# Unread products after each exposed recurrence step, with the last projection spread over four steps

## The reference, cut to what matters

```python
def step(carry, xs):
    h, c = carry
    xi_t, xf_t, xg_t, xo_t = xs
    i_t = jax.nn.sigmoid(xi_t + h @ V_i)
    g_t = jnp.tanh(xg_t + h @ V_c)
    o_t = jax.nn.sigmoid(xo_t + h @ V_o)
    c_new = h * c + i_t * g_t
    h_new = o_t * jnp.tanh(c_new)
    return ((h_new, c_new), h_new)
```

## Time and profile before

| | us |
|---|---|
| median of 3 runs (lowest, highest) | 839.23 (838.78, 840.98) |
| the profiled execution, its own time | 840.06 |
| its span, first to last instruction | 838.3 |
| PE busy, PEld busy | 688.0, 408.7 |
| DVE busy, ACT busy, POOL busy | 519.1, 372.2, 229.7 |
| chain that ended last | PE 57%, DVE 25%, ACT 8%, issue 5% |
| mean granted clock of TensorE | 0.851 |

### The profile page before, as it was taken

The page is one execution under the profiler, slowest core; times in us unless marked ns, Lnnn a source line. Parts: engine busy times, 40 slices in busy tenths (PEclk is TensorE's granted clock), DMA queues, the critical chain, the costliest instruction groups (busy, mean ns, idle before and its releaser), DMA issues.

```text
span 838.3 us, 16451 instructions
## 1 busy us (share of the span) xinstructions
PE 688.0 (82%) x6414; PEld 408.7 (49%) x6414; DVE 519.1 (62%) x1098; ACT 372.2 (44%) x693; POOL 229.7 (27%) x203
## 2 busy tenths in 40 slices
PE   3677778854579999988897899979899998787775
PEld 3674545633442222245233344246667775565553
DVE  3865775568956555366457666548776773465543
ACT  2232444431415456645444555545565654333332
POOL 4156754574600032111024110304332332000000
PEclk9989689866559999999999999988999998555555
DMA  9840000000025333200232132200000000000000
GB/s 184 144 80 10 1 1 1 2 0 1 0 99 173 103 128 124 72 2 7 79 106 67 61 98 81 60 1 2 2 2 2 2 2 1 11 10 9 11 10 12
DMA packets 42402, 36.85 MB, mean 44 GB/s; under 512 B 20888, under 2 KB 29848, under 8 KB 42328
## 3 DMA queue, kind: packets, MB, share of 16 engines
q1 hardware_dynamic: 41242, 35.57, 16.1%
q10 hardware_dynamic: 1088, 0.26, 0.2%
HBM read 33.85 MB, written 1.97 MB: 43 GB/s over the span
## 4 chain that ended last, share of the span: by engine, by line
PE 57%; DVE 25%; ACT 8%; issue 5%; POOL 2%; DMA 2%; ACTq 0%; DVEq 0%; SPq 0%; POOLq 0%
PE PS L1644 10%; PE PS L1631 10%; PE PS L1607 6%; PE PS L1679 3%; PE PS L1746 3%; PE PS L1735 3%; PE PS L1658 3%; DVE XC L980 3%; PE PS L1593 2%; PE PS L1700 2%; DVE st L962 2%; PE PS L1714 2%; ACT Y L696 2%; DVE st L978 2%; ACT LS L855 2%
## 5 line engine op out<-in xcount | busy, mean ns | idle before, releaser
L1644 PE MATMUL PS<-Y,W1f 64*128 64x512 f32 x384 | 111.5, 660 | 4.9 <-DVE Y L1121 2.8
L1631 PE MATMUL PS<-XC,w2s 128*64 128x512 f32 x384 | 105.8, 631 | 1.2 <-ACT BIG L732 1.2
L1607 PE MATMUL PS<-LS,V 64*64 64x32 f32 x1140 | 70.8, 270 | 36.1 <-DVE LS L1263 36.1
L1607 PEld LDWEIGHTS PS<-LS,V 64*64 64x64 f32 x1140 | 58.7, 188 | 70.6 <-DVE LS L1263 62.4
L741 ACT ACTIVATE XC<-PS 128x1024 f32<-128x1024 f32 x68 | 69.3, 1022 | 51.2 <-PE PS L1631 41.7
L600 POOL TENSOR_TENSOR st<-st,mhalf 128x8 f32<-128x8 f32 x12 | 21.6, 1796 | 194.1 <-DVE st L1108 194.1
L1121 DVE TENSOR_TENSOR Y<-XD,UF 128x512 f32<-128x512 f32 x96 | 65.3, 692 | 14.5 <-DMA UF<-gd 9.0
L1631 PEld LDWEIGHTS PS<-XC,w2s 128*64 128x64 f32 x384 | 19.6, 138 | 76.3 <-issue 66.6
L1250 DVE SCALAR_TENSOR_TENSOR LS<-LS 128x32 f32<-128x32 f32 x96 | 19.8, 206 | 57.5 <-ACT LS L849 39.7
L1644 PEld LDWEIGHTS PS<-Y,W1f 64*128 64x128 f32 x384 | 30.6, 190 | 50.1 <-issue 31.7
L178 POOL TENSOR_TENSOR st<-st,mhalf 128x8 f32<-128x8 f32 x24 | 39.3, 1639 | 36.6 <-DVE st L965 36.6
(11 more groups left out here) (236 smaller groups left out, 1437.5 us busy)
## 6 DMA issues: line engine op xcount, KB each, us to landing
UF<-gd SPq DMA_DIRECT2D x192, 128.0 KB, 2.9
BIG<-in_x SPq DMA_DIRECT2D x8, 512.0 KB, 12.7
out<-X SPq DMA_DIRECT2D x48, 32.0 KB, 2.0
W1f<-in_L_ffn_w SPq DMA_DIRECT2D x2, 512.0 KB, 6.3
EX<-in_L_ffn_w SPq DMA_DIRECT2D x1, 1024.0 KB, 15.1
H<-in_txt SPq DMA_DIRECT2D x2, 256.0 KB, 12.4
w2s<-in_L_ffn_w SPq DMA_DIRECT2D x1, 512.0 KB, 9.3
gd<-EX SPq DMA_DIRECT2D x6, 64.0 KB, 1.7
```

What stands on the lines that cost most here:

```text
L1607: mm = pe.matmul(PS[r, b, o:o + HN], V3[r, g, :], HB[r, (t - 1) % 4, :], start=False, stop=True, skip_group_check=True)
L1631: mm = pe.matmul(PS[64 * h:64 * h + 64, 6, :], w2s[:, 2 * p + h, :], Hb[:, n % 2 * 2 + h, :], start=(p == 0), stop=(p == E // 2 - 1))
L1644: mm = pe.matmul(PS[:, n % 2 * 2 + h, :], W1f[r, 2 * p + h, :], Rb[r, n % 4, :], start=True, stop=True)
```

## The change

It does these things:

- **Unread products.** At the end of PE's slot, for steps 32 to 94, one more fp32 product of 128 x 128 weights (`W1f`) with 256, 480, 176 or 272 columns (by t % 4), written to PSUM bank 0 or 1 and read by nobody. In the six steps in which PE also transposes a part of chunk 4 or 5, it is 288 columns shorter.
- **The last projection.** `project` in step 32 is replaced by one of its four products in each of steps 33, 37, 41 and 45 (`last_project`, bank 1), and `o_out` in step 32 by two halves in steps 46 and 47 (`last_out`).
- **Parts of chunks.** Chunks 4 and 5 begin at slots 114 and 130 (steps 49 and 65) in place of 108 and 124, with their parts spread further; chunk 3's last parts, the turn and the two copies, go from unit 26 to unit 24 of the attention. The parts of the last experts' chunk are spread otherwise over the first units.
- **Hidden steps.** They begin one slot later. On DVE `weigh` now comes between `cell` and `hidden`.
- **A wait.** In slot 50 PE's wait for the first attention's end comes behind `up`.

```diff
-        TAIL_DVE = {0: (2, 3, 4, 5), 1: (6, 7), 2: (8, 9), 3: (10,), 4: (11, 12), 5: (13, 14)}
-        TAIL_POOL = {1: ("pw0", "mu0", "ga"), 4: ("pw1", "mu1")}
-        TAIL_ACT = {1: 0, 4: 1}
+        TAIL_DVE = {0: (2, 3), 1: (4, 5), 2: (6, 7), 3: (8, 9, 10), 4: (11, 12), 5: (13, 14)}
+        TAIL_POOL = {2: ("pw0", "mu0", "ga"), 4: ("pw1", "mu1")}
+        TAIL_ACT = {2: 0, 4: 1}
...
-        LS0 = 3 * E + 10
+        LS0 = 3 * E + 11
...
-            if j == 1 and p in ("out", "t0", "t1", "k13", "k14"):
+            if j in (1, 4) and p in ("out", "t0", "t1", "k13", "k14"):
...
-        XB = (3 * E + 2, 3 * E + 13, None, None, NPR + 12, NPR + 28)
-        XALONE = dict(ao0=0, r0=0, q0=1, ao1=2, r1=2, q1=3, n0=4, n1=5, sq=6, n2=7, n3=7, pw=7, ones=8, mu=9, turn=10, c0=10, c1=11)
-        XLATER = dict(ao0=0, ao1=1, r0=0, q0=0, r1=1, q1=1, n0=1, n1=1, ones=2, sq=2, n2=3, n3=3, pw=3, mu=4, turn=5, c0=5, c1=5)
+        XB = (3 * E + 2, 3 * E + 13, None, None, NPR + 18, NPR + 34)
+        XALONE = dict(ao0=0, r0=0, q0=1, ao1=4, r1=4, q1=5, n0=6, n1=7, sq=8, n2=9, n3=9, pw=9, ones=10, mu=11, turn=12, c0=12, c1=12)
+        XLATER = dict(ao0=0, ao1=1, r0=0, q0=0, r1=1, q1=1, n0=2, n1=2, ones=3, sq=3, n2=4, n3=4, pw=4, mu=5, turn=7, c0=7, c1=7)
...
-              3: dict(ao0=16, r0=16, q0=16, ao1=20, r1=20, q1=20, n0=21, n1=22, sq=22, n2=23, n3=23, pw=23, mu=23, ones=24, turn=26, c0=26, c1=26)}
+              3: dict(ao0=16, r0=16, q0=16, ao1=20, r1=20, q1=20, n0=20, n1=21, sq=21, n2=22, n3=22, pw=22, mu=22, ones=23, turn=24, c0=24, c1=24)}
...
+        LAST_O = [XS + 1 + 4 * c for c in range(NP)]
+        LAST_C = [LAST_O[-1] + 1, LAST_O[-1] + 2]
...
+            def last_out(h):
+                R, G, b0 = UNITS[-1][0:3]
+                b0 = b0 // GA * GA + h * (GA // 2)
+                act.wait_ge(S("a_o"), G + 1)
+                act.activation(AO[:, :].rearrange("p (t b) -> p b t", b=NB)[:, b0:b0 + GA // 2, RB * R:RB * R + RB],
+                               PS[:, 1, 256 * h:256 * h + 256].rearrange("p (b i) -> p b i", i=RB), ACT.Identity, bias=bus[:, 0:1]).then_inc(S("o_ev"), 1)
...
-                if g == LS1:
-                    o_out(len(UNITS) - 1)
+                if t in LAST_C:
+                    last_out(LAST_C.index(t))
...
                 if t is not None:
                     cell(t)
+                if ahead <= g + 2 < NPR and not (g in AT or g + 1 in AT):
+                    weigh(g + 2)
+                if t is not None:
                     hidden(t)
                     if t % 4 == 1 and t > 4 and not begins(g - 1):
                         output(t // 4 - 1)
-                if ahead <= g + 2 < NPR and not (g in AT or g + 1 in AT):
-                    weigh(g + 2)
...
-                pe.wait_ge(S("o_ev"), 4 * (c // 2) + 4)
+                pe.wait_ge(S("o_ev"), 4 * (c // 2) + 4 + (c // 2 == NR - 1))
...
+            def last_project(c):
+
+                u, G = len(UNITS) - 1, NG - 1
+                mm = pe.matmul(PS[64 * (c % 2):64 * (c % 2) + 64, 1, :], NPt[:, c, :], Zs[G % 2][:, :, RB * c:RB * c + RB],
+                               start=(c < 2), stop=(c >= 2))
+                if c == NP - 1:
+                    mm.then_inc(S("a_o"), 1)
...
-                    if t == XS:
-                        project(NG - 1, len(UNITS) - 1, 2 * NG)
+                    if t in LAST_O:
+                        last_project(LAST_O.index(t))
...
+                if g >= LS1 and t < T - 1:
+
+                    n = (256, 480, 176, 272)[t % 4] - (288 if residual(g, "ao0", "ao1", "turn") else 0)
+                    b = 0 if t <= LAST_C[-1] + 1 else 1
+                    pe.matmul(PS[:, b, 0:n], W1f[:, 0, :], w2s[:, 0:8, :].rearrange("p e d -> p (e d)")[:, 0:n], start=True, stop=True)
```

More of the change, by code:

```diff
@@ L1576, in gates_x @@
                     if 4 * k == XS + 4:
-                        pe.wait_ge(S("o_ev"), NG)
+                        pe.wait_ge(S("o_ev"), NG - 1)
                     if k >= 2:
@@ L1841, in _ @@
                     pe.wait_ge(S("u_ev0"), 2 * G)
[L1842 to L1846, removed]
                 if t:
@@ L1853, in _ @@
                         out_tp(t // 4 - 1)
-                    if t == XS:
-                        project(NG - 1, len(UNITS) - 1, 2 * NG)
+                    if t in LAST_O:
+                        last_project(LAST_O.index(t))
                 if g < NPR and g not in (AT[0] + 1, AT[0] + 2):
                     up(g)
+                if g == AT[0] + 3:
+                    pe.wait_ge(S("z_ev0"), (JOBS[units_of(0)[-1] + 1] + 1) // 2)
+                    pe.wait_ge(S("z_ev1"), JOBS[units_of(0)[-1] + 1] // 2)
+                    pe.wait_ge(S("o_ev"), NB // GA)
                 if 2 <= g < NPR and not begins(g) and not begins(g - 1):
```

## The result

The changed kernel takes 845.22 us, median of 20 runs (838.68 to 850.29). The kernel before, beside it on the same chip, takes 839.39 us (835.49 to 846.10, 20 runs). The ratio is 1.0063, interval 1.0042 to 1.0084: slower by 0.6%. The ratios are of fast runs: those of the experiments leave out the profiled run and any that is more than 1.5% above the kernel's fastest. The profiled execution took 845.52 us, its span is 843.8 us.

What follows compares the result with a forecast made beforehand. The exposed steps were taken as bound by the chain, with PE's narrow products slowed at 1.2 GHz. The terms summed to +28.3, or 868.4 us; -6.6 for ten faster steps gave 862 us, range 821 to 870.

Steps and rivals of the forecast that it cites:

- rival B: Exposed steps: the clock alternates, half of the steps at each level, 846 us (835 to 855); chance 0.15.
- I expect the exposed part to start low, as it does now: Start of the exposed steps: the clock is at 1.2 GHz there, because the attention ends in a sparse stretch.
- I give them ten of the steps: Exposed steps: ten find the clock raised and cost about 1.71 us instead of 2.37, so -6.6 us.
- part 1: Chunk 3's turn and copies two units earlier: PE's wait at the start of the exposed part goes, -2.0 us.
- Part 3: Unread products at 1.2 GHz: they stand in front of the next gates, +28.4 us over 63 steps.
- Part 2: Projection out of step 32: the 5.21 us to the next h become an ordinary step, -3.3 us.
- Part 4: Four products of the last projection: +7.2 us at 1.2 GHz, +2.6 at 2.4 GHz.
- Part 5: Parts of chunks 4 and 5: their DVE and ACT work mostly hides in steps PE bounds, -1 us.
- Part 6: Hidden steps: `weigh` fills the gap in which DVE waits for ACT, -1 us.
- Rival A: Exposed steps: wide products lift the clock within the first steps and keep it, 823.8 us; chance 0.37.
- about six steps in ten: Share of exposed steps at 2.4 GHz below which losses in slow steps outweigh the gains.

Runs made afterwards that it cites:

- e10: The changed kernel with chunk 3's turn and copies back in unit 26 of the attention, as in the kernel before: 853.04 us, ratio 1.0218.
- e8: The changed kernel without unread products and with the last projection back in step 32 in one piece: 831.22 us, ratio 0.9918.
- e3: The changed kernel with unread products of half the columns (128, 240, 88, 136): 848.57 us, ratio 1.0103.
- e6: The changed kernel with longer unread products (352, 512, 272, 368 columns) and four more in steps 60, 62, 76 and 78: 823.24 us, ratio 0.9823.
- e5: The changed kernel with four more unread products, in steps 60, 62, 76 and 78, where PE idles longest: 831.73 us.
- e2: The changed kernel with unread products lengthened to 352, 512, 272 and 368 columns: 826.84 us.
- e1: The changed kernel without its unread products, all else kept: 832.18 us, ratio 0.9931.
- e4: The changed kernel with unread products in steps 32 to 57 alone: 830.57 us, ratio 0.9905.
- e7: e6 without the unread product in the four steps that also have a product of the last projection: 819.68 us, ratio 0.9778.

## Why the prediction was right and wrong

The time lay in the range and its sign was the forecast's, but not its size: 862 us, and +22 over the profiled execution of before, stand against 845.22 and +5.5. What came true is rival B, 846 us, to which I gave 0.15.

**The step that failed** is the one that says "I expect the exposed part to start low, as it does now", and with it the term "I give them ten of the steps". The part started at 2.4 GHz, and of the 63 steps 36 had it. I took the sparse end of the attention for the reason and had part 1 in the sum as -2.0 us of waiting; I did not ask what that wait did to the clock. The stretches of the kernel before show that the attention itself ends at 2.4 GHz:

```profile
690.00:700.00 10.00, 10.00 (x103) 7.48 (x102) 5.76 (x11) 6.46 (x8) 5.09 (x4) 1.00 0.00 0
703.80:707.50 3.70, 3.21 (x42) 0.54 0.00 0
```

(The second has no figures but PE's busy time.) From 702 to 704 the clock was still 1.00, with PE busy for 0.83 of 2.00 us around the wait; then it was low until the last projection was through the earlier trace rows. In e10, where the wait is back, the clock falls again as the exposed part begins, and in the changed kernel, without it, it doesn't. I also looked for what raises the clock, where the question was what holds it. At the prediction's own 0.66 us a step (2.37 less 1.71), 26 more steps at 2.4 GHz are 17 us, which would have made 845 of the 862. That this meets 845.22 so well is luck, since other terms were off as well.

**Part 3, the mechanism**, was right. At 1.2 GHz the unread products stand ahead of the gates and set the steps. The size was too small. I forecast 9.47 us for four steps; from the h of step 64 to that of step 88 it was 825.77 - 763.15 = 62.62 us, 10.44 for four. My price came from four products that ran two side by side, 3.5 ns a column with no fixed part. Alone, one takes 3.3 ns a column and 0.30 us. That is 1.2 us for four steps, less 0.2 for the cheaper columns: the 1.0 missing. With the clock low throughout the sum would have been 0.24 x 63 = 15 us further up. This error and that of the clock were of opposite sign.

**Part 1**: the h of step 32 came 4.06 us earlier, with 0.11 of it from before. 3.15 is the start of L1605; most of the rest is the gates at 2.4 GHz (0.78 us and not 1.47 from L1605's start to theirs). I had -2.0.

**Part 2**: step 33 fell by 3.52 us (forecast 3.3). But e8 shows that the split isn't the cause: the projection in one piece at 2.4 GHz leaves little to remove.

**Part 4**: +0.78 us for each of four steps at 2.4 GHz, forecast 0.64. At 1.2 GHz I had 1.80 each; in e3, which ran there, such a step took 3.77 us, 1.87 over the 1.90 of one with the same unread product alone.

**Part 5** held only at 1.2 GHz. There PE does bound the steps and the parts of chunk 5 mostly hide (steps 76 to 79 take 2.68, 2.45, 2.46 and 2.82 us, the four before them 2.69, 2.44, 2.68 and 2.72). At the higher clock they don't: 1.89, 1.84, 2.41, 1.68 and 2.03 us for steps 58 to 62. Worse, these steps are where the profiled execution lost the clock. Two of them in the timeline:

```profile
754.04 0.70 PE L1905 MATMUL PS<-w2s,W1f 128*128 128x256 f32 x2
...
755.63 0.54 PE L1619 MATMUL PS<-LS,V 64*64 64x32 f32 x12 [0.89 <-DVE LS L1274]
...
758.57 0.66 PE L1605 MATMUL PS<-XD,U 65*64 65x128 f32 x8 [0.66 <-DVE XD L1256]
```

**Part 6**: I forecast -1, and said that more than 3 us of change would refute it. The h of step 31 came at 532.13 instead of 532.24. But in the ten other profiles, whose kernels have the same hidden steps, it lies between 527.93 and 533.17, so two single profiles can't tell -1 from nothing.

**Rival B** named the course, with 36 and 27 steps at the two levels. Its 846 us is partly luck: it is halfway between two ends, of which the upper, 868, was 15 us too low.

**Rival A** (clock held, 16.3 us less than before) had the right price: e6, which holds it, runs 14.7 us under the kernel beside it, with unread products longer than A's, and the two runs of e5 that kept it 17 to 18. Its share of "about six steps in ten" as the turning point stands too: here 36 of 63 (0.57) had the higher clock, and the kernel is just on the slower side.

The Trainium skill, page "TensorE: Matmul & The Clock Gate", section "What's actually happening", has activity of the PE release the throttle; read as busy time, that would have lifted the clock here. The trace disagrees: with 68.07 of 68.10 us busy the clock stayed at 1.2 GHz before it rose, and in e3, with 134.31 of 136.00, it never rose.

What stays open is why the clock falls and rises where it does. In the changed kernel's 20 runs the mean clock was 0.877 to 0.900, and the time went with it: 838.68 us at 0.900, 850.29 at 0.877. One kernel thus loses the clock at differing places. Three profiles lost it near gaps (after, e2 and, both times, e10). But around steps 61 and 77 gaps, transposes and a shortened product stand together, and e5 lost it behind step 65, which has the last two with little idle time; whether idle time or too little wide work brings the fall was not separated. Once low, with much the same pattern of products, it stayed so for 7 and 10 us in e10 and then to the end, for 27 in e5, 34 in e2 and 68 in the changed kernel.

## What to carry over

Work that only keeps TensorE's clock up must be dense enough at the sparsest place of the stretch, and at its start: first take away the waits that lose the clock, then fill, and fill the sparse steps separately. Price it at the lower clock, with its fixed part: here a slow step lost 0.61 us and a fast one gained 0.19, so products that held the clock for 36 of 63 steps were worse than none (e1), and filling that stops early (e4) is better than filling that fails late. Where real wide products already stand in a step, the filler on top of them only costs (e7).

## What had not been expected of the hardware

A full-width float32 product that doesn't run beside another has a fixed part at 1.2 GHz: 0.66 us for 88 columns, 0.88 for 176 and 1.89 for 480 (at 2.4 GHz 480 take 1.00 us). And TensorE can be busy for 68.07 of 68.10 us, with 0.8 us of 64 x 64 products and some 0.9 to 1.9 us of full-width ones in every step, and stay at 1.2 GHz, while 8.6% of idle time (44.70 busy of 48.90 us in e4) didn't bring the higher one down. The busy shares of the two levels don't count the same work, since a product is under way for longer at the lower clock: the 68.10 us hold 562 instructions of PE, the 53.20 us at 2.4 GHz at the start 632.
